# Five chunks of three groups, two dense steps ahead of the last chunk's tiles, and a new order of scatters and gathers

## What is computed

```python
logits = x @ Wr + br;  probs = softmax(logits);  top_p, top_i = top_k(probs, 2)
cw = sum(one_hot(top_i, 8) * top_p)                 # weights of the two chosen experts
h = relu(x @ W1[e] + b1[e]);  y = h @ W2[e] + b2[e]
x = x + tanh(g_ffn) * sum_e cw[e] * y[e]
```

## Time and profile before

| | us |
|---|---|
| median of 3 runs | 798.38 |
| lowest, highest | 797.49, 798.66 |
| the profiled execution | 800.09 |
| its span in the trace | 798.4 |
| PE busy | 761.3 (95%) |
| DVE, ACT, POOL busy | 525.9, 497.8, 443.1 |

### The profile page before, as it was taken

How to read it: one execution, slowest core, us unless ns; L and a number is a source line. 1 busy time by engine, 2 the same in 40 slices (tenths; PEclk the granted TensorE clock), 3 DMA queues, 4 the chain that set the end, 5 groups by cost and what they waited for, 6 DMA issues and landing times.

```text
span 798.4 us, 17460 instructions
## 1 busy us (share of the span) xinstructions
PE 761.3 (95%) x5392; PEld 645.5 (81%) x5392; DVE 525.9 (66%) x1829; ACT 497.8 (62%) x1630; POOL 443.1 (55%) x455
## 2 busy tenths in 40 slices
PE   7999999999999999999999999999999999879788
PEld 7778777777888988788988788988878889768665
DVE  4636677685857567677658777767768556465536
ACT  3677767676866566766556576656568655445622
POOL 2233264646552444785656686565668465466663
PEclk9999999999999999999999999999999999999999
DMA  6745151542455542174654146575316456534523
GB/s 196 199 161 193 59 210 71 210 145 81 145 186 158 200 153 71 41 231 160 214 195 146 47 109 219 189 230 172 104 44 199 146 191 205 162 107 122 149 77 87
DMA packets 119791, 119.42 MB, mean 150 GB/s; under 512 B 14585, under 2 KB 94994, under 8 KB 119698
## 3 DMA queue, kind: packets, MB, share of 16 engines
q1 hardware_dynamic: 111088, 102.41, 39.0%
q0 software_dynamic: 7680, 15.74, 6.7%
q10 hardware_dynamic: 930, 0.15, 0.1%
HBM read 35.94 MB, written 41.55 MB: 97 GB/s over the span
## 4 chain that ended last, share of the span: by engine, by line
PE 79%; DVE 6%; issue 6%; ACT 4%; POOL 2%; another core or an unknown queue 2%; DMA 1%; SPq 1%; ACTq 0%; DVEq 0%; POOLq 0%
PE shared L1426 14%; PE batch L1364 12%; PE batch L1377 12%; PE hid_ps L1294 8%; PE xy_ps L1308 7%; PE batch L1372 6%; PE shared L1217 3%; PE shared L1219 3%; PE shared L1218 3%; PE batch L1308 2%; ACT probs L746 2%; PE xy_ps L1271 2%; PE batch L1354 1%; PE shared L1415 1%
## 5 line engine op out<-in xcount | busy, mean ns | idle before, releaser
L676 POOL TENSOR_TENSOR probs<-probs,rsums 128x512 f32<-128x512 f32 x128 | 132.9, 1038 | 234.3 <-DVE rsums L1147 232.0
L746 ACT ACTIVATE probs<-batch,neg_max 128x128 f32<-128x128 f32 x512 | 180.5, 374 | 2.0 <-DVE neg_max L1151 2.0
L651 POOL DMA_INDIRECT sorted_x<-xn,row_of x120 | 121.3, 1011 | 36.0 <-issue 28.0
L827 ACT ACTIVATE qT<-shared,tb 128x512 f32<-128x512 f32 x128 | 87.2, 696 | 85.4 <-PE shared L1219 75.8
L1377 PE MATMUL batch<-pT_sb,kvn 128*128 128x512 f32 x256 | 134.2, 606 | 5.5 <-ACT pT_sb L754 5.4
L1364 PE MATMUL batch<-kvT,qT 128*128 128x128 f32 x1024 | 135.4, 275 | 0.8 <-ACT qT L827 0.8
L1426 PE MATMUL shared<-M,oT 128*128 128x128 f32 x1024 | 125.3, 275 | 0.2
L1364 PEld LDWEIGHTS batch<-kvT,qT 128*128 128x128 f32 x1024 | 124.4, 192 | 1.2 <-ACT qT L827 1.2
L1426 PEld LDWEIGHTS shared<-M,oT 128*128 128x128 f32 x1024 | 119.5, 192 | 1.3 <-issue 1.3
L746 ACT ACTIVATION_READ_ACCUMULATOR probs<-batch,neg_max 128x1 f32 x512 | 110.3, 215 | 0.0
L761 ACT ACTIVATE oT<-batch 128x512 f32<-128x512 f32 x128 | 76.2, 595 | 47.6 <-PE batch L1377 42.6
(11 more groups left out here) (168 smaller groups left out, 1241.7 us busy)
## 6 DMA issues: line engine op xcount, KB each, us to landing
wt<-wall SPq DMA_DIRECT2D x124, 321.0 KB
sorted_x<-yg SPq DMA_DIRECT2D x36, 512.0 KB, 4.9
xt<-sorted_x SPq DMA_DIRECT2D x162, 64.0 KB
sorted_y<-y_sb SPq DMA_DIRECT2D x78, 128.0 KB
kv<-in_ctx_dram SPq DMA_DIRECT2D x16, 256.0 KB
kv<-in_x_dram SPq DMA_DIRECT2D x16, 256.0 KB
xres<-in_x_dram SPq DMA_DIRECT2D x32, 128.0 KB
out_dram<-x SPq DMA_DIRECT2D x15, 256.0 KB
```

The source lines that it names most:

```text
L651: nc.gpsimd.indirect_dma_start(xs[k % SETS][:, :], bass.IndirectOffsetOnAxis(ap=row_of[:, g, choice, c:c + 1], axis=0), xn[:, g % 2, c, :] ...
L676: nc.gpsimd.tensor_tensor(pv, pv, rsums[:, m % 2, :].unsqueeze(2).broadcast_to([P, 4, P]), ALU.mult).then_inc(probs_ready, 1)
L746: last = nc.scalar.activation(probs[:, m % 2, c * P:(c + 1) * P], batch_ps[m % BANKS][:, c * P:(c + 1) * P], ACT.Exp, bias=neg_max[:, m % ...
L827: nc.scalar.activation(qT[:, g % 2, :, number, :], sh[:, :].rearrange("p (b i) -> p b i", b=GB), ACT.Identity, bias=tb[:, number:number + ...
```

## The change

`CHUNKS` becomes (3, 3, 3, 3, 3): 80 tiles, T64 to T79 at slots 139 to 154. The last chunk holds groups 12 to 14. Dense steps 0 and 1 move to slots 133 and 134, with other PSUM banks, and steps 2 to 7 follow the tiles at slots 155 to 160; `BIAS_SLOT` is 140. Group 14 is scattered at slots 130 and 131, two columns each. `gather_room` deals the gathers behind slot 131: two in a slot right behind a dense step, one in a tile's slot (two in every fourth), four a slot from 156 on. So groups 9 to 11 are gathered at slots 134 to 154, groups 12 to 14 at 156 to 161, and all their combines are at slots 145 to 164. The last group's gathers have a semaphore for each half, and `combine_last` adds them half by half; SP stores the halves one by one, and the dense group ahead of them. Waits are set to the new order: dense step 0 waits for xT, step 1 for the shared banks, step 2 for the biases, and T64's output for the adds of dense steps 0 and 1.

```diff
-CHUNKS = (3, 3, 3, 3, 2, 1)
+CHUNKS = (3, 3, 3, 3, 3)
+SCATTER_LAST = (2, 2, 3, 3)
-DENSE_SLOT = [LAST_TILE + 1 + e for e in range(E)]
+EARLY = 2
+DENSE_SLOT = [TAIL + 2 + e if e < EARLY else LAST_TILE + 1 + e - EARLY for e in range(E)]
+def gather_room(n):
+    if n < TAIL:
+        return GATHERS.get(n % GB, 0)
+    if n > LAST_TILE + 1:
+        return 4
+    if n - 1 in DENSE_SLOT:
+        return 2
+    return (1 + (TILE_AT[n] % 4 == 3)) if n in TILE_AT else 0
 def gather_slots():
...
-        n = max(n, TILE_SLOT[FIRST_TILE[CHUNK_OF_GROUP[g] + 1] - 1] + 3)
+        n = max(n, TILE_SLOT[FIRST_TILE[CHUNK_OF_GROUP[g] + 1] - 1] + (2 if last else 3))
...
-        if g < LATE_GROUP + 2:
-            summed.append(n + LANDED)
-        elif g < SORTED - 1:
-            summed.append(max(n + LANDED - 1, summed[-1] + 1, DENSE_SLOT[g - LATE_GROUP - 1]))
-        else:
-            summed.append(max(n, summed[-1] + 2, DENSE_SLOT[-2]))
+        summed.append(n + (2 if last else LANDED))
-BIAS_SLOT = GB * (G + 1) + 2
+BIAS_SLOT = TILE_SLOT[LATE] + 1
@@ SP, behind the loop: the last sorted group in halves, the dense group at DENSE_SLOT[-1] + 2
+                if n == DENSE_SLOT[-1] + 2:
+                    for half in range(2):
+                        sp.wait_ge(dense_step, E + 1 + half)
+                        store_half(DENSE, half)
             for half in range(2):
-                sp.wait_ge(dense_step, E + 1 + half)
...
+                sp.wait_ge(res_done, SORTED + half)
+                store_half(SORTED - 1, half)
@@ POOL
-                                             ).then_inc(gathered[BUFFER[g]], 16)
+                                             ).then_inc(gathered_last[c // 2] if g == SORTED - 1 else gathered[BUFFER[g]], 16)
...
-                if s in SCATTER and 0 <= g < SORTED:
-                    scatter_rows(g, SCATTER.index(s))
+                for c in range(4):
+                    if 0 <= g < SORTED and s == (SCATTER if g < SORTED - 1 else SCATTER_LAST)[c]:
+                        scatter_rows(g, c)
@@ DVE
+            def combine_last():
+                g = SORTED - 1
+                for half in range(2):
+                    dve.wait_ge(gathered_last[half], 16 * 4)
+                    for choice in range(2):
+                        for c in (2 * half, 2 * half + 1):
+                            last = nc.vector.scalar_tensor_tensor(out=x1[:, g, c, :], in0=outputs_of(g)[:, c, choice, :],
+                                                                  scalar=share[:, g, choice, c:c + 1], in1=x1[:, g, c, :], op0=ALU.mult, op1=ALU.add)
+                        last.then_inc((part_done, res_done)[choice], 1)
+                        if choice == 0:
+                            dve.wait_ge(part_done, SORTED + half)
@@ PE
 def output_tile(i):   # the branch for i >= LATE
                     pe.wait_ge(o_out, B)
+                    pe.wait_ge(dense_step, EARLY)
 def dense_hidden(e):
                 if e == 0:
-                    pe.wait_ge(dense_step, 1)
+                    wait_shared(pe, shared_out, "turn_x", DENSE, 0)
+                    pe.wait_ge(o_out, B)
                 elif e == 1:
+                    for bank in range(2):
+                        pe.wait_ge(shared_out[bank], shared_uses[bank])
+                elif e == EARLY:
+                    pe.wait_ge(dense_step, EARLY + 1)
+                elif e == EARLY + 1:
                     pe.wait_ge(xtT_done, N_TILES)
```

More of the change, by code:

```diff
@@ L136, in gather_slots @@
     for g in range(SORTED):
-        n = max(n, TILE_SLOT[FIRST_TILE[CHUNK_OF_GROUP[g] + 1] - 1] + 3)
+        last = CHUNK_OF_GROUP[g] == NCH - 1
+        n = max(n, TILE_SLOT[FIRST_TILE[CHUNK_OF_GROUP[g] + 1] - 1] + (2 if last else 3))
         for h in in_buffer(BUFFER[g], g - 1)[-1:]:
@@ L140, in gather_slots @@
         for what in [(g, c, choice) for c in range(4) for choice in range(2)]:
-            while True:
-                if n >= TAIL:
-                    room = 0 if n % GB in SCATTER and n <= GB * (G + 1) else 2
-                else:
-                    room = GATHERS.get(n % GB, 0)
-                if len(at.get(n, ())) < room:
-                    break
+            while len(at.get(n, ())) >= gather_room(n):
                 n += 1
@@ L351, in dense_hid, with added @@
         def dense_hid(e, c):
-            return (shared[c], (xy_ps, batch_ps[1])[c])[e % 2]
+            if e < EARLY:
+                return (batch_ps[c], shared[c])[e]
+            return (shared[c], (xy_ps, batch_ps[1])[c])[(e - EARLY) % 2]
         def dense_y(e):
-            return batch_ps[2 + (N_TILES + e - LATE) % 2]
+            return batch_ps[2 + (e if e < EARLY else N_TILES + e - EARLY - LATE) % 2]
+        def added(e):
+            return e + 1 + (e >= EARLY)
         turned = [xy_ps, hid_ps]
@@ L565, in store_tile, with store_half @@
                 sp.dma_start(rows_of.rearrange("(a p) d -> p a d", p=HALF), y_sb[:, i % 2, 0:PARTS[i], :]).then_inc(y_stored[i % 2], 16)
+            def store_half(g, half):
+                at = slice(GB * g + 4 * half, GB * g + 4 * half + 4)
+                sp.dma_start(out[at, :, :].rearrange("(c b) s d -> (b s) c d", b=2), x1[:, g, 2 * half:2 * half + 2, :]).then_inc(stored, 16)
             for n in range(FIRST, LAST + 1):
@@ L1125, in add_dense @@
             def add_dense(e):
-                dve.wait_ge(dense_step, e + 1)
+                dve.wait_ge(weight_step, 2)
+                wait(dve, dense_step, added(e) - 1)
                 dve.wait_ge(dense_y_ready, e + 1)
@@ L1204, in add_up @@
                 for g in COMBINE_AT.get(n, ()):
-                    combine(g, 0)
+                    if g < SORTED - 1:
+                        combine(g, 0)
+                    else:
+                        combine_last()
                 for g in SECOND_AT.get(n, ()):
-                    combine(g, 1)
+                    if g < SORTED - 1:
+                        combine(g, 1)
                 add_biases(n)
@@ L1314, in dense_biases @@
                 if n == BIAS_SLOT:
-                    for bank in range(2):
-                        pe.wait_ge(shared_out[bank], shared_uses[bank])
+                    pe.wait_ge(dense_hid_out, EARLY)
                     pe.wait_ge(weight_step, 2)
```

26 lines of the change are left out of this document (14 added, 12 removed).

## The result

The changed kernel takes 800.50 us (median of 12 runs, 798.86 to 802.37), the kernel before 797.27 us in the same comparison (12 runs, 795.99 to 798.66). The ratio is 1.0039, interval 1.0028 to 1.0050: 3.2 us slower. The forecast was 796.6, range 789.5 to 805.5, and faster by 0.1%. The time lies in the range, the sign is wrong.

The account below looks back on a forecast made before the run. Tiles paced by gathers that hold PE's signals, then PE's dense steps, were taken to set the end. T79's output at 755.7, its store to 758.5, gathers 33, then 1.3 + 1.2 + 2.6 gave 796.6 us, range 789.5 to 805.5.

Parts of the forecast that it names:

- the signs: Tail: hidden matmuls near 2.2 us apart, POOL's last 24 gathers without pause over 2 us, PE idle from before 786.
- the tile stretch: PE from T64's hidden to T79's output: 34.7 us alone plus 2.4 for neighbours, 37.2 us in the sum.
- the store: Behind T79's output, its rows reach memory before group 12's gathers: 2.8 us with y_sb's add.
- the gathers: 24 gathers of groups 12 to 14 behind the last tile, the new end: 33 us, between 30.0 and 36.3.
- the end: Behind the last gather: data 1.3, second half of combine_last 1.2, store 2.6 us.
- The allowance of 2.4 us for neighbours: Tile stretch: extra for ACT and DVE being nearly as busy as PE's 2 us slot; bounds 0 and 15 us.
- the overlap: Behind the tiles: dense steps 2 to 7, 21 us of PE, lie beside the 24 gathers and no longer count.
- rival D: Behind the tiles: dense steps held through the gathers end at 790, under the gathers; no price or chance of its own.
- until it is through: Tiles of the kernel before: a run of four gathers holds PE's signals back until the run ends.
- A: Tiles and late gathers: signals stay held, slots 2.5 us, gathers 36.3 us; 804.5 us, slower; chance 0.27.
- B: Whole tail: nothing is held, T64 at 717, PE stretch 34.7, gathers 30.5; 790.2 us; chance 0.22.
- C: Late gathers: lengthened by combines beside them, 37.9 us instead of 33; 801.5 us; chance 0.1.

Follow-up runs that it names:

- e6: The changed kernel unchanged, run again for its profile beside the kernel before (778.27 us): 793.01 us, ratio 1.0186.
- e5: The kernel before, unchanged, run again for its profile: 778.03 us, ratio 0.9999.
- e4: Kernel before with only the new gather dealing; old chunks, dense slots, scatters and stores kept: 787.44 us, ratio 1.0118.
- e10: Kernel before with only the new gather dealing, old chunks kept, repeated on another chip: 787.97 us, ratio 1.0114.
- e13: Kernel before with only the new gather dealing, old chunks kept, on one more chip: 786.70 us, ratio 1.0118.
- e9: Changed kernel with gathers of groups 9 to 11 dealt as before, two a slot behind 131 without scatters: 792.80 us, ratio 1.0175.
- e11: The changed kernel unchanged, run once more as a level on another chip: 792.06 us, ratio 1.0166.
- e12: Changed kernel with ten extra matmuls filling TensorE's wait for xn ahead of the dense group's transposes: 791.66 us against 792.06.

## Why the prediction was right and wrong

*Right.* The time, 800.5, lies within the range, the tile slots are near the 2.2 us that the signs asked for (2.22 from T66 to T79), and no wait "remote" stands in the tiles. The gathers come at 1.25 us. Here is the tail of the changed kernel's POOL; the first of the last 24, then the two that end pauses, then the last:

```profile
757.14 0.94 POOL L687 DMA_INDIRECT yg<-sorted_y,home  x1 [4.72 <-DMA sorted_y<-y_sb]
...
779.42 0.94 POOL L687 DMA_INDIRECT qT<-sorted_y,home  x1 [2.35 <-remote]
...
785.94 0.94 POOL L687 DMA_INDIRECT qT<-sorted_y,home  x1 [1.83 <-remote]
...
789.74 0.95 POOL L687 DMA_INDIRECT qT<-sorted_y,home  x1 [0.30 <-issue]
```

Sixteen run unbroken, then come the pauses. One is over the 2 us that the signs allowed, and PE still works at 789.9, where the signs had it idle from before 786.

*Right by luck.* T64's hidden was forecast to start 36.5 us after the last scores' start (718.5) and started at 36.7 (715.77), but not by the path of the forecast. That had the last scatter end at 28.4 us, signals held for 1.6 us around it and 6 us for the loads. Measured, the last scatter ends at 26.0, nothing is held between 691 and 774 us, dense output 1 is over at 34.2, and yet T65's rows land only at 36.4. SP issues the loads at 31.9, behind an output store that waits for a combine behind the logits:

```profile
707.44 0.19 DVE L1005 TENSOR_TENSOR logit<-shared,br_all 128x32 f32<-128x32 f32 x1 [3.93 <-PE shared L1483]
...
707.99 1.13 DVE L1133 SCALAR_TENSOR_TENSOR x<-yg,share,x 128x128 f32<-128x128 f32 x4
...
709.15 0.38 SPq L615 DMA_DIRECT2D out_dram<-x  x1
710.99 7.87 SPq L553 DMA_DIRECT2D xt<-sorted_x  x12
...
715.50 0.44 PE L1313 MATMUL batch<-ident,xt 128*128 128x128 f32 x2 [1.50 <-DMA xt<-sorted_x]
```

The prediction had neither this store nor the router product on the way to T64. What moving the store would bring, no run shows.

*The terms that were off*, forecast and measured: the tile stretch 37.2 and 38.4; the store 2.8 and 2.95; the gathers 33 and 33.55; the end 5.1 and 6.6; T64 0.2 late (T79's output counted to 754.2, by PE's pace, as in the prediction; the table has the modelled end). Together 3.6 us, and each of them small: the sign hung on a forecast gain of 1.8. In the tiles the slots are 2.0 us, as in the earlier trace rows, but for one:

```profile
742.00 1.06 PE L1351 MATMUL batch<-wt,hs 128*128 128x128 f32 x8
744.62 0.44 PE L1313 MATMUL batch<-ident,xt 128*128 128x128 f32 x2 [1.56 <-DMA xt<-sorted_x]
```

```profile
744.21 0.42 DVE L1236 TENSOR_TENSOR y_sb<-batch,wt 128x256 f32<-128x256 f32 x1 [3.21 <-DMA sorted_y<-y_sb]
```

The allowance of 2.4 us for neighbours was spent on the start (T65 waits 1.5 us for its rows, matmuls of 1.35 and 1.91 us at the lower clock) and on one late load, beside a late store.

*The step that failed* is the overlap: "the dense steps 2 to 7 [...] lie beside it and no longer count", and with it rival D's "it changes nothing, and has no price of its own". PE had finished the dense hidden matmuls by 770, but its signals were held through most of the gathers. PE's output of step 5, then DVE of the changed kernel:

```profile
766.40 1.95 PE L1402 MATMUL batch<-wall,qT 128*128 128x128 f32 x16
```

```profile
762.57 1.13 DVE L1133 SCALAR_TENSOR_TENSOR x<-yg,share,x 128x128 f32<-128x128 f32 x4
774.35 1.13 DVE L1173 SCALAR_TENSOR_TENSOR x<-batch,weight,x 128x128 f32<-128x128 f32 x4 [10.65 <-remote]
...
784.36 1.13 DVE L1173 SCALAR_TENSOR_TENSOR x<-batch,weight,x 128x128 f32<-128x128 f32 x4 [7.84 <-remote]
...
790.45 2.31 DVE L1133 SCALAR_TENSOR_TENSOR x<-qT,share,x 128x128 f32<-128x128 f32 x8
792.67 2.44 DVE L1144 SCALAR_TENSOR_TENSOR x<-qT,share,x 128x128 f32<-128x128 f32 x8
```

The product of 766.40, over by 768.35, is added at 784.36, 16 us later; in e6 the same product is over at 766.86 and added at 766.99. The chain that ended last runs through these adds and their waits and through no gather of the last 24:

```profile
761.52 1.13 DVE x L1173 x4
762.65 1.04 DVE x L1133 x4
763.70 10.53 another core or an unknown queue
...
776.52 7.72 another core or an unknown queue
...
784.36 1.13 DVE x L1173 x4
...
793.31 1.15 DVE x L1144 x4
```

That is the sign that the prediction itself gave for being wrong, the chain ending in dense steps. The add at 774.35 also shows that a signal can arrive in the middle of a run of sixteen gathers (757.14 to 777.08), so "until it is through" doesn't hold as stated.

DVE takes instructions in order, and the dense adds stand ahead of the combines. From 784.36 to 795.11 it has work all the time but for 0.8 us. With the last adds pushed to 789.9, level with the last gather, the combines of groups 13 and 14 come in one unbroken row, 4.7 us from 790.45 to 795.11; they end 4.4 us behind the last gather, where 2.5 us (the data and one half) were forecast. So the last two terms of the sum can be measured, but here they are not what set the end. The same stretch of e6, where nothing is held:

```profile
772.58 1.12 DVE L1173 SCALAR_TENSOR_TENSOR x<-batch,weight,x 128x128 f32<-128x128 f32 x4
777.29 2.31 DVE L1133 SCALAR_TENSOR_TENSOR x<-qT,share,x 128x128 f32<-128x128 f32 x8 [3.59 <-DMA qT<-sorted_y,home]
782.71 1.26 DVE L1144 SCALAR_TENSOR_TENSOR x<-qT,share,x 128x128 f32<-128x128 f32 x4 [3.10 <-DMA qT<-sorted_y,home]
787.05 1.26 DVE L1144 SCALAR_TENSOR_TENSOR x<-qT,share,x 128x128 f32<-128x128 f32 x4 [3.07 <-DMA qT<-sorted_y,home]
```

Here DVE waits for gathered rows, one half of 1.26 us remains, last gather to end is 5.3 us (forecast 5.1), and the chain that ended last runs through POOL's gathers. From the last tile's output to the end the changed kernel takes 42.9 us with the hold and 38.0 in e6: the hold's price there is 4.9 us, which the prediction had at nothing beyond its 3 us of waits among the gathers. The other 2.3 us of the 7.2 between the two tails lie ahead of that, where the profile has one held signal (DVE at 691.0, 2.69 us; the last scatter ends at 26.0 us against 24.1 in e6) and a late load; how they share the 2.3 us is not shown. In the kernel before the two profiles differ by 20.9 us in the tail (116.4 against 95.5), and the medians by 19.2: 4.6 up to T64's hidden matmuls, the rest up to T83's output.

*The starting point.* The prediction said that a run of four gathers holds PE's signals and took that for a property of the kernel. On the four chips of the experiments it isn't, and there the change costs 13 to 15 us. Why, e5 and e6 show: in e5 the dense steps set the end (last add at 92.9, end at 95.5) and the last gather is over at 86.7; in e6 it is over at 105.7 and sets the end. Of these 19.0 us 8.7 are the last tile's, which itself ends later, and the rest comes from 24 gathers (29.85 us) that wait for the last tile, where e5 has 16 left from 747.37 on (19.8 us). That the measured loss was only 3.2 us means that the hold cost the changed kernel less than the kernel before: 7.2 us of tail against 20.9. This last split is a comparison between sets of runs; the hold was not met again, so it is not shown by an experiment that the dealing cures it. The first comparison's own tile slots speak for it (2.22 us from T66 to T79, against 3.10 from T66 to T83), but the chunks changed with it. e4, e10 and e13 were made to part the two and met no hold.

*The rivals.* A had one half right: at the late gathers the hold stayed, in the tiles it did not. B is what the chips of the experiments do (its terms: gathers 30.5, measured 29.85), but its gain was reckoned from a kernel before with the hold. D came in its premise, and its price was not nothing. C did not come: combines lie beside the gathers from 762.57 on, and the 24 gathers take 0.94 to 1.13 us each; in e5 28 of them take 0.94 to 1.12. The long gathers of the earlier trace rows did not come back. The Trainium skill, page "SBUF — State Buffer", section "Who interferes with whom", has a DVE instruction with two SBUF inputs contend with a GpSimd instruction that reads SBUF, and calls the shared ports an exclusive lock; its words "fully blocks" stand with DVE's two-port modes. These 52 gathers were lengthened by 0.19 us at most, so they don't show one blocked for the length of a combine (1.13 us).

## What to carry to other kernels

Count what stands behind the last producer: an indirect gather cost GpSimd 1.25 us from start to start in every run here, and a last chunk of three groups puts 24 of them after its last row; seven half tiles saved did not pay for it. A stall whose cause the trace doesn't name ("remote") is a weak base for a forecast: run the kernel before once more elsewhere, if that can be had, before building on it. On an engine that works in order, work held up ahead of the last steps is paid at the end, even when the last steps don't need its results; so ask of every wait you call free what stands behind it. And follow a load back through what its queue has ahead of it: here an output store ahead of T64's loads tied them to a router product.

## What the runs showed of the hardware

The same kernel took 797.3 us in one comparison and 777 to 779 us on four chips, 2.4% apart, at a granted clock of 0.991 and 1.000 in the profiled executions; 20.9 us of it lie in a tail of 116 us. In the slow one some of TensorE's completed work is seen by the other engines late while GpSimd issues indirect DMAs: by 3 us for T78's hidden matmuls, by 16 us for the product of 766.40. In the thirteen other profiles no such wait stands behind 685 us. Beside it, behind a gap of 4.3 us without matmuls the granted clock fell to its lower level: it was 0.50 for all of 700 to 710 us in e6, e9 and e11, and 0.59 to 0.77 in the others, with 1.00 from 710 us on in four of them; with the gap filled (e12) it stayed at 1.00.
